# The opening of the layer-1 expert stage: two copies of weights issued ahead of the second group's row loads, and the fourth expert's weights loaded after those rows

## The reference, cut to what matters

```python
logits = x @ router_w                      # x: layer-normed, 2048 x 512
scores = sigmoid(logits)                   # groups, top 4 groups, top 8 experts of 32
tkw = 2.5 * (scores of the 8) / (their sum)
xs = repeat(x, 8)[sorted by expert]
gate, up = xs @ w_gate[e], xs @ w_up[e]    # 512 -> 256 each
down = (silu(gate) * up) @ w_down[e]       # 256 -> 512
routed[row] = sum over its 8 experts of tkw * down
out = x + routed + shared expert
```

## Time and profile before

| | us |
|---|---|
| Time, median of 3 runs | 2993.95 (2988.72 to 2998.57) |
| The profiled execution's own time | 2994.6 |
| Its span, first to last instruction | 2992.8 |
| TensorE busy | 2622.1 (88%) |
| VectorE busy | 1535.3 (51%) |
| GpSimd busy | 1294.2 (43%) |
| ScalarE busy | 1032.8 (35%) |

### The profile page before, as it was taken

How to read it: one execution, slowest core, us unless ns; L and a number is a source line. 1 busy time by engine, 2 the same in 40 slices (tenths; PEclk the granted TensorE clock), 3 DMA queues, 4 the chain that set the end, 5 groups by cost and what they waited for, 6 DMA issues and landing times. The chain is left out here.

```text
span 2992.8 us, 41291 instructions
## 1 busy us (share of the span) xinstructions
PE 2622.1 (88%) x11315; PEld 1086.1 (36%) x11318; DVE 1535.3 (51%) x2654; ACT 1032.8 (35%) x1305; POOL 1294.2 (43%) x933
## 2 busy tenths in 40 slices
PE   5888976699999987768999999798099999999998
PEld 1343432244444433323333333443033333333333
DVE  7999999631110032136666564731045555555554
ACT  4646564120000011023443333200055555555553
POOL 2767656312300032116565633146535455545554
PEclk8999999999999999889999999899599999999999
DMA  3433222310210289982067100254657776787764
GB/s 127 116 96 105 86 64 71 123 50 22 86 33 14 80 283 353 287 216 82 1 175 195 42 1 1 73 217 187 207 137 158 160 155 121 139 219 158 161 119 61
DMA packets 361887, 372.82 MB, mean 125 GB/s; under 512 B 85810, under 2 KB 268403, under 8 KB 361778
## 3 DMA queue, kind: packets, MB, share of 16 engines
q1 hardware_dynamic: 202210, 239.03, 25.4%
q0 software_dynamic: 45520, 93.26, 14.7%
q10 hardware_dynamic: 114048, 39.16, 5.9%
HBM read 231.96 MB, written 152.14 MB: 128 GB/s over the span
## 5 line engine op out<-in xcount | busy, mean ns | idle before, releaser
L1874 POOL DMA_INDIRECT out_x<-e_yo,e_dest x288 | 418.7, 1454 | 411.0 <-DMA out_x<-e_yo,e_dest 281.4
L2092 PE MATMUL e_psg<-e_wgu,e_xsT 128*64 x1152 | 519.9, 594 | 83.0 <-ACT e_cgu L1947 83.0
L2092 PE MATMUL e_psg<-e_cgu,e_xsT 128*64 128x512 f32 x1152 | 519.9, 594 | 0.0
L287 POOL TENSOR_TENSOR hc<-hs,bcst 128x1024 f32<-128x1024 f32 x128 | 300.8, 2350 | 179.6 <-DVE ps_b L507 170.6
L1947 ACT ACTIVATE e_cgu<-e_wgu 128x2048 f32 x144 | 275.1, 1911 | 133.0 <-issue 130.6
L632 PE MATMUL ps_y<-hc,ident 128*128 128x512 f32 x512 | 241.2, 609 | 89.4 <-POOL hc L287 89.2
L513 DVE TENSOR_TENSOR_SCAN hs<-dA,ps_b 128x1024 f32<-128x1024 f32 x128 | 292.7, 2286 | 8.1 <-ACT dA L417 3.9
L2092 PEld LDWEIGHTS e_psg<-e_wgu,e_xsT 128*64 128x64 f32 x1152 | 154.2, 137 | 332.0 <-issue 332.0
L2114 PE MATMUL e_pso<-e_wd,e_hT 128*64 x576 | 270.7, 592 | 0.7 <-DVE e_hT L2014 0.7
L2114 PE MATMUL e_pso<-e_cd,e_hT 128*64 128x512 f32 x576 | 270.7, 592 | 0.0
L1237 PE MATMUL r_ps_t<-r_wd,r_h 128*128 128x512 f32 x480 | 210.7, 600 | 9.6 <-DVE r_h L984 5.1
(11 more groups left out here) (426 smaller groups left out, 4202.3 us busy)
## 6 DMA issues: line engine op xcount, KB each, us to landing
slots_in<-zeros SPq DMA_DIRECT2D x144, 256.0 KB
e_xs<-slots_in ACTq DMA_DIRECT2D x144, 256.0 KB
bcst<-bc_rows SPq DMA_DIRECT2D x128, 256.0 KB, 4.2
e_wgu<-in_wg SPq DMA_DIRECT2D x32, 512.0 KB
e_wgu<-in_wu SPq DMA_DIRECT2D x32, 512.0 KB
e_wd<-in_wd SPq DMA_DIRECT2D x32, 512.0 KB
e_w<-in_wg SPq DMA_DIRECT2D x11, 1408.0 KB
e_w<-in_wu SPq DMA_DIRECT2D x11, 1408.0 KB
```

Of the source, the lines that this page charges most:

```text
L287: pool.tensor_tensor(hc[:, it % 2, half(h), :], hs[:, it % 2, half(h), :], bc(bcst[:, q, 1, :], 1, HB), ALU.mult).then_inc(sem["hc"], 1)
L1874: pool.indirect_dma_start(out[:, :], bass.IndirectOffsetOnAxis(dest[:, q, s:s + 1], 0), yo[half(s), q, :], None, bounds_check=T + 2 * P - ...
L2092: j = pe.matmul(ps_g[half(s), q % 2, :], xsT[:, q % 2, k, half(s)], w, start=k == 0, stop=k == KH - 1, tile_position=(0, s * HALF), skip_g ...
```

## The change

On ScalarE the two copies of weights for tiles 0 and 1 go ahead of the second group's row and record loads. On SyncE a wait is put between the announcements of the first three experts and the loop: the first refill, the fourth expert's, is issued once the second group's rows have landed.

```diff
@@ expert_stage1, SyncE
                 for s in range(AHEAD):
                     announce(s, 0)
+                sp.wait_ge(rows_in[1], 16 * NQ)
                 with sp.Fori(0, E // RING - 1) as i:
                     for q in range(RING):
                         refill(i * RING + q, q)
@@ expert_stage1, ScalarE
-                for r in range(2):
-                    load_rows(r * RING * P, r)
-                    load_rec(r * RING * P, r)
+                load_rows(0, 0)
+                load_rec(0, 0)
                 act.wait_ge(sem["ids"], 1 + 16)
                 copied(0, 0)
                 copied(1, 1)
+                load_rows(RING * P, 1)
+                load_rec(RING * P, 1)
                 for t in range(OUT):
                     gate(t, t)
```

## The result

| | before | after |
|---|---|---|
| Time, median of 9 runs, us | 2993.95 (2988.17 to 2998.57) | 2987.88 (2982.72 to 2993.02) |
| Ratio of after to before, 95% interval | | 0.9977 (0.9967 to 0.9986) |
| Ratio when measured once more (10 runs and 14) | | 0.9973 (0.9964 to 0.9983) |
| Span of the profiled execution, us | 2992.8 | 2987.3 |

The forecast was 2985.3 us, 8.7 us less, with a range of 2980 to 2991. The medians differ by 6.1 us; the two ratios are 6.9 and 8.1 us of 2994, with intervals from 4.2 to 10.8. So the time is in the range and the gain a little under the forecast, within 0.3% of before.

A forecast was written before the change was run, and what follows sets the result against it. The last stage's start bounded the kernel, through ScalarE's load issues ahead of the first weight copy. Starting 8.7 us earlier, with other costs 0, took the profiled 2994.6 to 2985.9, less 0.65 for a median of 2985.3 us; range 2980 to 2991.

The forecast's parts named there:

- The bound and the one-for-one rule: Last stage: TensorE's matmuls run unbroken from 2177 to 2977 us, so moving their start moves the kernel's end equally.
- The copies: ScalarE, opening: first copy of weights starts at 2158.90, letting TensorE start at 2161.13, 9.4 us earlier.
- The rows: First group's rows land earlier: VectorE starts at 2160.4, TensorE at 2161.8 instead of 2170.53, 8.7 us earlier.
- the lag: From the first group's last packets to VectorE's start: 1.7 us before, 0.9 to 1.7 after, taken as 1.3.
- rows as late as now: Lower bound at the opening: first group's rows unchanged, TensorE starts at 2163.9, a gain of 6.6 us.
- The case of the rivals in which the rows stay at +9.15: First group's rows come no earlier than before: gain 6.6 us, time 2987.3, chance 0.17.
- The second group's issues: ScalarE, behind the copies: issued from 2160.0 to 2164.2, length between 4.17 and 9.36 us, cost 0 at gate(0).
- The rivals that went by 9.36 us or by issues of 2.64: Second group's issue on ScalarE delays gate(0): 2987.2 to 2989.9 us, chance 0.13; or, at 2.64 each, 2996.3, chance 0.04.
- SyncE's refills: SyncE: fourth expert's weights issued near 2167, wanted near 2222, slack above 35 us, cost 0.
- The clock: TensorE, tile 0: 4.2 us at the lower clock before; no difference taken for the change.
- The bounds that I had set, 3.4 to 7.0: Length of tile 0 in us with all eight matmul pairs at the high or the low clock; 5.68 seen.
- The total: Whole kernel: 8.7 us less, median 2985.3 us; chance 0.58 within 0.3% of before, 0.39 faster, 0.03 slower.

The follow-up runs named there:

- the two halves of the change: Only ScalarE's reordering, or only SyncE's wait, put into the kernel before: ratios 0.9981 and 0.9991 of before.
- the identity matmuls: 16 TensorE matmuls ahead of the first tile, added to the change with tile 0's rows (0.9955 of before) or tiles 0 and 1 (0.9962) loaded first.
- tile 0 alone: The change, with tile 0's rows in four loads of their own ahead of the copies and the second group behind gate(0): 0.9955 of before.
- copies alone: The kernel before with only ScalarE's reordering, SyncE loading the fourth expert at once: 0.9981 of before.
- waiting for the first group: The change, but SyncE waits for the first group's rows instead of the second's: 0.9976 of before.
- early weights: The change, plus 1 MB of weights loaded by SyncE into an unused tile right behind the list of experts: 0.9986 of before.

## Why the prediction was right

**The bound and the one-for-one rule: right.** The stage behind silu 0 is 816.3 to 816.6 us long with and without the change, which is the claim of a closed run. (The 82.96 us in the earlier trace rows are TensorE's whole idle stretch, most of it ahead of the stage; within the stage it stood 17.2 us.)

**The copies: right.** Forecast +5.55 (2158.90 less 2153.35), measured +5.35; the second copy at +7.17.

**The rows: right in the sum, by two errors that cancel.** Forecast start of the transposition +7.05, first matmul +8.45; measured +7.20 and +8.51.

```profile
2164.02 1.10 DVE L2011 STREAM_TRANSPOSE e_xsT<-e_xs 128x512 f32<-128x512 f32 x1 [3.58 <-DMA e_xs<-slots_in]
```

The rate held as well: q10 moves 1337 packets in three microseconds without q1, 446 in each where 435 was taken, and the earlier trace rows have 551 in three with it. (The three from 2158 lie earlier in the stage here than in the earlier trace rows.)

```profile
q10 hardware_dynamic: 1337, 0.67, 100.2%
```

But the packets that I counted up to 2048 were not all rows: by 2161, 68 of q10's 2092 were small ones, under 512 B. Taken from the same trace without them, the last row packet of before ends at +8.35, not near +7.45, so VectorE starts 0.8 us behind it and not 1.7. With q1 silent the last one was to be through at +5.85, and the lag was taken as 1.3, from a range of 0.9 to 1.7. After the change the packet ends at +6.40 (+6.42 in the second profile) and the lag is 0.8. The packets were forecast 0.55 us too early and the lag 0.5 too long. That the sum comes within 0.15 us is luck.

And the bound "rows as late as now" was one draw of an event that varies. A second profile of before had the rows at +7.45. The case of the rivals in which the rows stay at +9.15 could thus not be read off one profile. The prediction made the rows 2.1 us earlier; they were so by 1.95 us in the first pair of profiles and by 0.24 in the second, and SyncE's wait itself has at most 1.5 of it. On the gain this hardly bears, since in the kernel before the copies were far behind the rows either way.

**The second group's issues: right.** 3.2 us, below the 4.17 that I took, and no cost at gate(0). The rivals that went by 9.36 us or by issues of 2.64 are out: those lengths came with q1 and with the first group ahead of them, as the two halves of the change show (5.2 us without q1 and right behind the first group, 7.3 and 6.6 with q1 and the first group nearly through).

**SyncE's refills: right.** First refill at +14.67, where 2167 (+13.65) was forecast; no hole at tile 4 or at the fourth expert. SyncE's queue after the change, the first refill and the one of the slot of expert 0:

```profile
2171.49 0.61 SPq L1773 DMA_DIRECT2D e_wgu<-in_wg  x1
...
2183.47 0.55 SPq L1773 DMA_DIRECT2D e_wgu<-in_wg  x1
```

**The clock: no difference between the first profiles, as taken, but the term is not constant, and that it came out even is luck.** Tile 0 took 5.70 and 5.58 us, and 5.05 to 6.63 over all kernels without the identity matmuls; before varies as much (5.70 and 6.63). The bounds that I had set, 3.4 to 7.0, hold all of them.

**The total.** The stage gained 9.0 us in the first pair of profiles, 8.7 of it at the first matmul, and 9.4 in the second, 8.2 of it there and 1.0 by the clock in tile 0; 8.7 was forecast. The timed medians gave 6.1, and the two ratios 6.9 and 8.1. Both intervals hold 0.9970, which is 9.0 us of 2994. That the rest is scatter of the stages ahead is likely, not shown: of the ten timed comparisons (the stage of before taken as 839.7), seven gained 1 to 2.3 us less in time than in their stage, and three as much or more (tile 0 alone 13.5 against 10.8). These ten share four sets of runs of before, though, and the three are just those of one set, so they are no ten independent signs of a cost. A cost of 1 to 2 us outside the stage can't be excluded by these runs.

## What to carry to other kernels

Issuing a DMA occupies the engine that issues it, and for long if earlier packets are still queued: here 9.4 us for six loads of 1.1 MB. Order an engine's opening by who is waited for first, and issue what is needed later behind the work that everybody waits for, if its slack can be counted in tiles. Where an unbroken run of matmuls follows, count the stage from its own first instruction and not by the span. Loading the first tile by itself before the rest of its group took another 1.6 us off the stage here, in one profile.

## What the runs showed of the hardware that I had not expected

- **SyncE's first packet comes later when ScalarE is issuing too.** The weights' first packet came 1.4 us after SyncE's issue when ScalarE had issued nothing for the last 4.5 us or more (after: issued 2171.49, the first of q1's packets at 2172.9; the same in six more profiles). It came 2.2 to 3.4 us after it when SyncE issued at +2.0, amid ScalarE's six loads (before: packets at +4.2 and +5.1; copies alone: +5.5 and +4.2), or during the last of them (waiting for the first group: issued +8.61, packets at +11.8). Only the early weights, issued at +0.35, took 1.6. It went with this delay, about 1 us more or less, whether the weights met the first group's rows. What causes it, and why it varies, stays open.
- **Packets are shared evenly, bytes are not.** In the run with early weights q1 moved 752 packets with 0.75 MB and q10 734 with 0.36 MB in the same four microseconds. The rows, in pieces of 512 B, got half of the packets and a third of the bytes; alone they went at about 445 packets a microsecond (1337 in three), 0.22 MB.
- **The low clock's length varies.** Without the identity matmuls tile 0 took between 5.05 and 6.63 us at the same work, because its granted clock rose early or late in it. Against the 3.70 us of a tile all at the high level, and with pairs twice as far apart at the low one, that is an estimate of 2.7 to 5.9 us at the low level; the profiles' own record of the clock has it rise 2.8 to 5.9 us after the first matmul. A change of 1 us in this opening can't be read from one profile without looking at this.
